# Four ends of one gated cross-attention and expert kernel: gate loads on another queue, early transposes, loops written out, routed tiles begun among shared outputs

## The reference, cut to what matters

```python
# x (32,112,256), ctx (32,375,128); 16 heads of 64; 14 routed experts (top 2) and 2 shared, 256-512-256
x = x + tanh(g_xattn) * (attention(layernorm(x), ctx; Wq, Wk, Wv, Wo) + bo)
xn = layernorm(x)
gates = softmax(xn @ router_w); keep the top 2, divided by their sum
ffn(e) = silu(rmsnorm(xn) * rms_w[e] @ w1[e]) @ w2[e]
x = x + tanh(g_ffn) * (sum over kept experts of gate * ffn(e) + ffn_s(0) + ffn_s(1))
```

## Time and profile before

| | |
|---|---|
| median of 3 runs | 1460.05 us |
| the profiled execution, its own time | 1458.97 us |
| its span, from the first to the last instruction | 1457.2 us |
| PE busy | 1435.2 us, 98% of the span |
| DVE, ACT, POOL busy | 1081.7, 935.1, 463.4 us |
| mean granted TensorE clock | 0.999 |
| the chain that ended last, share of PE | 95% |

### The profile page before, as it was taken

One profiled execution on the slowest core, in us unless ns is written; L12 is line 12 of the kernel. 1 busy time (PEld: TensorE's weight loads), 2 busy tenths in 40 slices (PEclk: granted clock), 3 DMA queues, 4 the chain that ended last, 5 costly groups with the idle time before them and its releaser, 6 DMA issues.

```text
span 1457.2 us, 31992 instructions
## 1 busy us (share of the span) xinstructions
PE 1435.2 (98%) x9774; PEld 1346.5 (92%) x9774; DVE 1081.7 (74%) x2614; ACT 935.1 (64%) x2398; POOL 463.4 (32%) x688
## 2 busy tenths in 40 slices
PE   7999999999999999999999999999999999999998
PEld 7999999999999999999999999998789978888888
DVE  4878888888888888888788888878587444444448
ACT  6777777777776777777777777776453345455452
POOL 4313142231323413143231332417100145555520
PEclk9999999999999999999999999999999999999999
DMA  4010311213112131211303112150022346662235
GB/s 125 7 51 17 115 74 51 95 31 114 76 49 79 50 108 38 93 74 55 107 15 116 74 49 85 44 191 32 28 102 116 142 168 237 213 236 85 78 130 213
DMA packets 55583, 137.07 MB, mean 94 GB/s; under 512 B 10496, under 2 KB 38160, under 8 KB 51920
## 3 DMA queue, kind: packets, MB, share of 16 engines
q1 hardware_dynamic: 48880, 118.01, 23.4%
q0 software_dynamic: 6624, 18.13, 3.9%
HBM read 86.69 MB, written 49.43 MB: 93 GB/s over the span
## 4 chain that ended last, share of the span: by engine, by line
PE 95%; DVE 2%; ACT 1%; issue 1%; DMA 0%; SPq 0%; ACTq 0%; DVEq 0%
PE bank L586 19%; PE bank L587 18%; PE bank L588 18%; PE bank L647 10%; PE bank L1702 7%; PE bank L1045 6%; PE bank L1037 5%; PE bank L1722 4%; PE bank L1726 2%; PE bank L1712 2%; PE bank L1689 1%; PE bank L1218 1%; PE bank L602 1%; DVE pT_lo L855 1%; DVE nmax L872 0%
## 5 line engine op out<-in xcount | busy, mean ns | idle before, releaser
L763 ACT ACTIVATE prob<-bank,nmax 128x375 f32<-128x375 f32 x448 | 258.8, 578 | 190.3 <-DVE nmax L872 188.3
L855 DVE TENSOR_TENSOR pT_lo<-bank,pT_hi 125x384 fp32r<-125x384 f32 x448 | 246.2, 550 | 25.3 <-ACT pT_hi L774 23.7
L872 DVE TENSOR_REDUCE nmax<-bank 128x1 f32<-128x375 f32 x448 | 241.3, 539 | 29.9 <-PE bank L588 28.6
L647 PE MATMUL bank<-keep_ident,prob 128*125 128x128 f32 x1344 | 221.0, 273 | 0.9 <-DVE prob L881 0.9
L774 ACT CAST pT_hi<-bank 125x384 fp32r<-125x384 f32 x448 | 212.6, 475 | 1.7 <-PE bank L647 1.7
L647 PEld LDWEIGHTS bank<-keep_ident,prob 128*125 128x125 f32 x1344 | 201.4, 187 | 6.9 <-DVE prob L881 1.2
L586 PE MATMUL bank<-attend_wvo_hi,zT_hi 128*112 128x256 f32 x512 | 169.4, 331 | 0.7 <-DVE x L916 0.7
L586 PE MATMUL bank<-pT_hi,kv_hi 125*128 125x448 f32 x384 | 152.8, 398 | 4.3 <-DVE zT_lo L855 1.6
L586 PE MATMUL bank<-attend_kvT_hi,qp_hi 128*128 128x376 f32 x448 | 152.0, 339 | 1.4 <-ACT prob L763 1.3
L587 PE MATMUL bank<-attend_kvT_hi,qp_lo 128*128 128x376 f32 x448 | 149.8, 334 | 0.0
L588 PE MATMUL bank<-attend_kvT_lo,qp_hi 128*128 128x376 f32 x448 | 149.0, 333 | 0.0
(11 more groups left out here) (238 smaller groups left out, 3724.8 us busy)
## 6 DMA issues: line engine op xcount, KB each, us to landing
w_split<-we_split SPq DMA_DIRECT2D x14, 2048.0 KB, 6.9
keep_weights<-w_split SPq DMA_DIRECT2D x14, 2048.0 KB
we_in<-in_w SPq DMA_DIRECT2D x28, 512.0 KB, 5.9
keep_y_all<-y_rows SPq DMA_DIRECT2D x14, 512.0 KB, 9.1
kv_in<-in_ctx SPq DMA_DIRECT2D x32, 187.5 KB
h_rows<-hrow SPq DMA_DIRECT2D x32, 112.4 KB, 2.3
keep_h_in<-h_rows SPq DMA_DIRECT2D x7, 514.0 KB, 9.3
x_in<-in_x SPq DMA_DIRECT2D x16, 224.0 KB, 2.8
```

The lines of the kernel that those rows point to most:

```text
L647: last = nc.tensor.transpose(turn_bank_of(s)[0:MP, c * P:(c + 1) * P], prob[:, s % NB, c * MP:(c + 1) * MP], ident[:])
L763: nc.scalar.activation(prob[:, s % NB, :], score_bank(s)[:, 0:M], ACT.Exp, bias=nmax[:, s % NB:s % NB + 1], accum_out=psum_[:, s % NB:s % ...
L855: return nc.vector.tensor_tensor(dst, src, hi.bitcast(F32), ALU.subtract)
L872: nc.vector.tensor_reduce(nmax[:, s % NB:s % NB + 1], score_bank(s)[:, 0:M], AX, ALU.max, negate=True).then_inc(max_ready, 1)
```

## The change

- SP no longer loads the gates; ACT issues these two loads ahead of its tanh, and SP begins with x.
- PE gets 20 turns of the identity into bank 7 (`warm`), as soon as the identity is written and before it waits for Wk.
- The hardware loops of PE, DVE, POOL and SP are written out pair by pair.
- In the last pair POOL does `scale_shared` ahead of `ln2_root(29)`. The splits stay where they were.
- `turn(pe, 1)` goes one step of the attention's tail earlier.
- At the end of `front` PE's order becomes: turn rows 0, output part 0, turn rows 1, part 1, routed hidden 0, part 2, routed hidden 1, turn rows 2, part 3. ACT's and DVE's parts of rows 1 and 2 move with them. The banks of the turned hidden rows and of the routed outputs change places, since banks 4 and 5 still take shared outputs then.
- The last group's store goes out in two halves of 256 KB, each when its two parts are added.

```diff
-        def sync_gates(sp):
+        def sync_gates(act):
...
+        def warm(pe):
+            pe.wait_ge(ident_ok, 1)
+            for _ in range(20):
+                nc.tensor.transpose(banks[7][:, 0:P], sb["ident"][:], sb["ident"][:])
...
-            body(0, FULL)
-            with eng.Fori(1, PAIRS - 1) as p:
-                body(p, FULL)
-            body(PAIRS - 1, LAST)
+            for p in range(PAIRS):
+                body(p, LAST if p == PAIRS - 1 else FULL)
...
             split_context(p, 1)
+            sb["scale_shared"](pool)
             ln2_root(2 * p - 1)
             add_bias(p, 1)
-            sb["scale_shared"](pool)
...
-            for s in range(last_tile(7) + 4, last_tile(7) + 6):
-                behind(last, s, (), True)
+            behind(last, last_tile(7) + 4, (), True)
             sb["turn"](pe, 1)
-            for s in range(last_tile(7) + 6, last_tile(7) + 9):
+            for s in range(last_tile(7) + 5, last_tile(7) + 9):
...
-            sb["turn_first_rows"](pe)
-            output(len(items) - 1)
+            sb["turn_rows"](pe, 0)
+            output(len(items) - 1, (0,))
+            sb["turn_rows"](pe, 1)
+            output(len(items) - 1, (1,))
+            sb["routed_hidden"](pe, 0)
+            output(len(items) - 1, (2,))
+            sb["routed_hidden"](pe, 1)
+            sb["turn_rows"](pe, 2)
+            output(len(items) - 1, (3,))
...
-            sb["split_first_rows"](dve)
-            for t in range(4):
+            sb["split_rows"](dve, 0)
+            sb["split_rows"](dve, 1)
+            for t in (0, 1):
+                accumulate(len(items) - 1, t)
+            sb["split_rows"](dve, 2)
+            for t in (2, 3):
                 accumulate(len(items) - 1, t)
...
-        HT_BANK, H_BANK, T_BANK, O_BANK = banks[0:2], banks[2:4], banks[4:6], banks[6:8]
+        HT_BANK, H_BANK, T_BANK, O_BANK = banks[0:2], banks[2:4], banks[6:8], banks[4:6]
...
-            for g in range(BEFORE, GROUPS):
+            for g in range(BEFORE, GROUPS - 1):
                 sp.wait_ge(acc_done, 4 * (g - BEFORE) + 4)
                 store(g)
+            g = GROUPS - 1
+            for t in (0, 2):
+                sp.wait_ge(acc_done, 4 * (g - BEFORE) + t + 2)
+                sp.dma_start(by_group(io["out"], g)[:, t:t + 2, :], acc[:, 4 * g + t:4 * g + t + 2, :]).then_inc(out_stored, 16)
```

More of the change, by code:

```diff
@@ L210, in fuse_weights @@
         return {"sync_gates": sync_gates, "sync_keys": sync_keys, "sync_values": sync_values, "gpsimd": gpsimd,
-                "gpsimd_bias": gpsimd_bias, "turn": turn, "fuse": fuse, "copy_turned": copy_turned, "tanh": scalar_tanh,
+                "gpsimd_bias": gpsimd_bias, "warm": warm, "turn": turn, "fuse": fuse, "copy_turned": copy_turned, "tanh": scalar_tanh,
                 "split_hi": split_hi, "split_lo": split_lo, "copy_whole": copy_whole, "split_four": split_four}
@@ L469, in sync @@
             body(0, FULL)
-            with sp.Fori(1, PAIRS - 2) as p:
+            for p in range(1, PAIRS - 2):
                 body(p, FULL)
@@ L566, in gpsimd @@
             body(0, True)
-            with pool.Fori(1, PAIRS - 1) as p:
+            for p in range(1, PAIRS - 1):
                 body(p, False)
@@ L694, in tensor @@
             Q0, Q1, Q2, Q3 = (Q[u] for u in range(4))
+            weights["warm"](pe)
             for i in range(6):
@@ L792, in ln2_roots @@
                 nc.scalar.activation(rs2[:, 2, :], rs2[:, 1, :], ACT.Exp, scale=-0.5).then_inc(ln2_act, 1)
+            weights["sync_gates"](act)
             weights["tanh"](act)
@@ L1249, in hidden, with output @@
                     shared_hidden(nc, sb, g, e, j, H_BANK[j]).then_inc(h_done, 1)
-            def output(i):
+            def output(i, parts=range(4)):
                 e = items[i][1]
                 pe.wait_ge(hid_lo_ok, 4 * i + 4)
-                for t in range(4):
+                for t in parts:
                     if e == 0 and items[i][0] > 0 and t % 2 == 0:
@@ L1691, in turn_rows, with part, hidden @@
             last.then_inc(h_turned, 1)
-        def tensor(pe):
[L1694 to L1704, removed]
+        slots = {}
+        def part(slot, at, n):
+            return weights[:, bass.ds(slot, 1), at:at + n].rearrange("p s n -> p (s n)")
+        def hidden(pe, t):
+            b = t % 2
+            slot = slots[t] = pe.value_load(ring_of[0:1, t:t + 1], min_val=0, max_val=RING - 1)
+            pe.wait_ge(hT_lo, t + 1)
+            for k in range(2):
+                for q, (a, at) in enumerate((("hi", 0), ("lo", 0), ("hi", HID))):
+                    last = nc.tensor.matmul(H_BANK[b][:, :], hT[a][:, b, k, :], part(slot, 2 * k * HID + at, HID),
+                                            start=k == 0 and q == 0, stop=k == 1 and q == 2)
+            last.then_inc(hid_done, 1)
+        def tensor(pe):
             def turn_hidden(t):
@@ L1730, in tensor @@
             pe.nop(nofuse=True).then_inc(o_done, 1)
[L1731 to L1736, removed]
+            for t in range(1, SLOT_TILES + 2):
+                if 2 <= t < SLOT_TILES:
+                    hidden(pe, t)
+                if 3 <= t + 1 < SLOT_TILES:
                     turn_rows(pe, t + 1)
-                if 1 <= t <= SLOT_TILES:
+                if t <= SLOT_TILES:
                     turn_hidden(t - 1)
@@ L1772, in scalar @@
             rows_hi(0)
+            rows_hi(1)
             for t in range(SLOT_TILES + 2):
@@ L1809, in vector @@
                     second_half(t - 2)
-        sb["turn_first_rows"] = lambda pe: turn_rows(pe, 0)
-        sb["split_first_rows"] = lambda dve: rows_lo(dve, 0)
+        sb.update(turn_rows=turn_rows, routed_hidden=hidden, split_rows=rows_lo)
         return {"sync": sync, "gpsimd": gpsimd, "tensor": tensor, "scalar": scalar, "vector": vector}
```

12 lines of the change are left out of this document (5 added, 7 removed).

## The result

The changed kernel takes 1465.04 us (median of 11 runs, 1463.68 to 1471.72) against 1459.51 before (11 runs): ratio 1.0047, 95% interval 1.0032 to 1.0062. The forecast was 1453.8, with 0.04 for slower; the loss is more than twice the 0.2% that the prediction took for the least it could tell. Three of the eleven runs took 1471.4 to 1471.7; none of them has a profile, and what they add is left open. The profiled execution took 1464.63 us.

A forecast was written before the change was run, and what follows sets the result against it. PE was taken as the bound, busy 1435.2 of 1457.2 us. Savings of 1.8 + 0.4 + 1.5 + 0.85 + 1.7 + 0 = 6.25 us from 1458.97 gave 1452.7, as median 1453.8; range 1450.2 to 1456.6.

The forecast's parts named there:

- Start: Before the first fused product: loads issued 0.92 us earlier and 20 early turns save 1.8 us, bounds 0.5 to 2.4.
- The step on the clock: At the start: 20 early turns raise PE's clock by 6.2 us, so 24 real turns cost about 2.7 instead of 4.9.
- rival 4: At the start: early turns do not raise the clock in time, or wait; start gives 0.5, total 1455.1 us; 10%.
- Loops: Pairs written out: the seam loses 0.08 us for each of 14 pairs, 1.1 us if code is the reason; 0.4 taken.
- rival 2: Loops over the pairs did cost: writing them out saves 3.8 us instead of 0.4, total 1450.4 us; 12%.
- PE's pace inside a pair is its matmuls': In the loops over pairs: matmuls set PE's pace; only the seam's 0.08 us a pair could be saved.
- Shared weights scaled earlier: Last pair on POOL: scaling in idle time removes 2.7 us of DVE waits, 1.2 come back; saves 1.5, bounds 3.0 and -0.5.
- lines 931 and 932 now meet splits (POOL instructions up to 2.50 us): Last pair: these DVE lines meet splits instead of scalings; waits at 993 to 1004 can put 1 us or so back onto PE.
- rival 1: Last pair: POOL's work only changes places, splits block DVE as dearly; the 1.5 us are lost, total 1455.3 us; 18%.
- Routed tiles begun among the shared outputs: Change to routed tiles: of 2.73 us lost between turns and hidden, 1.7 are saved, bounds 0.8 and 2.7.
- the wait that stays: Change to routed tiles: `turn_hidden(0)` waits for all 20 additions, 0.76 us, 0.96 with the hand-overs.
- Rival 3: Written-out pairs: long streams are not fed in time and stop PE or DVE; at 1 us a pair 1467.8 us; 5%.

The follow-up runs named there:

- the run with empty instructions: The changed kernel with one empty instruction ahead of each of POOL's eight splits of the shared weights: 1466.05 us.
- the one with the copy ahead of the bias: The changed kernel with a 128x512 copy on POOL and a wait for it ahead of the last pair's bias: 1466.42 us.
- the run with the old order: The changed kernel with POOL's scaling of the shared weights put back behind the norm of batch 29: 1454.06 us, ratio 0.9962.
- The last kernel: The changed kernel with real gaps between the eight splits, gates on SP, and PE's wait for shared additions moved to the first routed output: 1451.26 us, ratio 0.9941.
- half a row: The changed kernel with the second shared expert's four splits moved behind the norm of batch 30 on POOL: 1463.15 us.

## Why the prediction was wrong, point by point

**Start, forecast -1.8, measured +0.38: wrong in its step "all of SP's loads go out 0.92 us earlier ... 0.92 earlier 8.65".** They did go out earlier, but landed no sooner: with the 20 turns alone PE could begin on the second half of Wq at 10.12 us, with the issue as in the earlier trace rows, and in the changed kernel, issued 0.93 sooner, at 10.60, where 8.65 was forecast. It is no accident of one profile: the second half of Wq landed at 10.3 to 11.0 us in the twelve profiles with the early issue and the gates on ACT's queue, and at 9.5 to 10.4 in the six with the old order on SP. That the rate of the transfers ahead of it sets its landing is the likely reason; no run tests it alone. The step on the clock came out in this kernel: the 24 turns of Wk and Wq have a median of 272 and 273 ns. "On ACT they cost nothing" was wrong as well: the gates landed at 7.24, ACT's norm work went from 6.7 to 8.78, and DVE's line 910 from 8.36 to 10.43, ahead of its copies of the turned Wq in the queue. Nor do the 20 turns keep their promise each time, which is rival 4: in five of the fifteen profiles that have them the turns of Wk, of Wq or of both had a median of 377 to 421 ns. In the run with empty instructions the granted clock was 0.50 from 10 to 12 us and the first fused product came at 12.94; in the one with the copy ahead of the bias it was 0.50 there too, and the product came at 12.41.

**Loops, forecast -0.4, measured -3.8: the term was mis-sized, and rival 2 (12%) gave its size, 3.8.** The step that failed is "PE's pace inside a pair is its matmuls'". At the seam the prediction's 0.08 us a pair was right, though only 0.4 of the 1.1 us that it makes was taken. By the starts of the score matmuls within a pair, 0.08 of the 0.30 us comes at the seam, 0.18 from 15 to 20 us behind the transposes of x, just after DVE's lines 931, 932 and 881 have met POOL's expert splits (line 931 takes 0.92 us in a loop and 0.64 without; POOL begins these splits 0.2 us sooner there), and 0.04 just behind the transposes. Busy time could not show it: in the stretch from 15 to 20 us PE is busy for 5.00 of 5.00 us in both kernels. The prediction's sign of being wrong, spacings that change by more than 0.1 us, came true. The Trainium skill (Runtime: NRT & Kernel Launch, Instruction fetch mechanics) had the sign right; that fetching is the cause no run here shows. How POOL's and DVE's meeting there makes PE's 0.18 is read from their places alone.

**Shared weights scaled earlier, forecast -1.5 with bounds of -3.0 and +0.5, measured about +11: the step that failed.** It is "lines 931 and 932 now meet splits (POOL instructions up to 2.50 us)": the cost of meeting POOL was bounded by one POOL instruction, as every row of before showed it. What the bound left out is which instruction stands ahead of the splits. In the old order the scaling stood between the bias and the splits; now the first split, at 990.02, follows the bias without a gap. (The forecast had it at 992.6; the last pair began 3.4 us sooner, so against its start the split came 0.8 us late.) DVE then missed every changeover. Of the 11.1 us over the run with the old order, PE idled 12.0 and lost some 1.9 at half clock (matmuls from 1004.10 to 1008.05 that take 2.0 us at full clock); the waits of the old order that fell away are the other side. The forecast's own fear, ACT late for `ln2_root(29)`, did not come true: the scaling ran from 973.93 to 985.96, and line 791 ran without a wait. With gaps between all splits the stage took 100.52 and 101.11 us in two runs, 1.15 and 0.56 less than in the old order without gaps, against 1.5 forecast. The old order with gaps was not run, so the move's own share of that is not known. Where DVE was let in but the row had no or one gap, it took 0.4 to 2.0 us more than with the old order; that is rival 1, and the likeliest case had been put ahead of it.

**`turn(pe, 1)`, forecast -0.85:** the stage is 102.50 us with the loops written out alone and 101.67 with the old order on POOL in the changed kernel: -0.83. Right.

**Routed tiles begun among the shared outputs, forecast -1.7, measured -1.29.** The mechanism was right, and so was the wait that stays; what was missed is the 0.41 us at the next hidden (1178.78), whose split on DVE stands behind the same additions in DVE's order. The last kernel gets 1.52 us more.

**Store in halves, forecast 0, measured +0.08.** Right.

**Rival 3**, slower through long streams, falls: spacings got shorter, and the loops written out alone gain 0.3%. The kernel is slower through a mechanism that no rival named, and 1465.04 lies 8.4 us above the range. (The range's lower end, 1450.2, is given as rival 2's, which comes to 1450.4; nothing hangs on it.)

Shown are: the long wait is made by POOL's row and lasts to its end (half a row, 6.0 us); one gap of 0.08 us inside it ends it, one ahead of it prevents it; and all seven profiles with the long wait, none of the eleven without, have a row without a gap that begins right behind the bias (with the moment kept, 0.9 us against 13.0). Why it does this, while the norm's small product or a scaling ahead of the row does not, stays open. That the bias reads two SBUF operands is not enough: so does the row's fourth split, which the fifth follows without a gap, and with the bias ahead of the norm the scaling that asked 0.18 us behind the sixth split's start, at 997.67, was in after 1.07 us; another DVE instruction had got in at the changeover to the fifth.

## What to carry to other kernels

A POOL instruction's length does not bound what it costs DVE: where POOL runs instructions back to back, put a real wait on the one before between them, some 0.1 us each, which here turned a loss of 0.5% into a gain of 0.4%. The empty instruction made no gap here; look at the starts. And read a stream's loss by the starts of its instructions, not by busy time in a window, and do not carry a shift of a transfer's issue over to its landing.

## What the runs showed of the hardware

- A DVE scaling of 128x375 in SBUF was kept out through six or seven changeovers of POOL, 12.3 to 13.0 us, in the changed kernel and in five experiments (and to the end of half a row, 6.0 us, in a sixth), each time in a row that began right behind the bias; in the other ten experiments it took 2.1 us at most.
- Weights issued 0.93 us sooner, with two loads of 0.5 KB on ACT's queue instead of ahead of them on SP's, landed no sooner (second half of Wq at 10.3 to 11.0 us in twelve profiles, 9.5 to 10.4 in six). The two small loads took 4.0 and 6.0 us beside the large ones, 2.3 and 2.7 at the head of SP's queue.
- Twenty early turns had the next 24 at the fast pace (medians of 272 and 273 ns) in ten of fifteen profiles.
- Written-out pairs were 0.30 us shorter each than a hardware loop's, 0.18 of it just behind the place where DVE meets POOL's splits.
